# Neighbour features gathered by edge block ahead of the edge loop, scores of two slots in one VectorE instruction

## The chip, the core and the metric

The kernel runs on one core of a Trainium2 chip. The engines are TensorE (PE, with its weight loads PEld), VectorE (DVE), ScalarE (ACT), GpSimd (POOL) and SyncE (SP); SP, ACT and POOL issue DMAs, the indirect ones (gathers by a list of indices) come from POOL. The metric is the device time of one execution in microseconds (us).

## The reference

A graph of 3125 nodes with 16 features each and 100000 edges, sorted by destination. The first layer makes two 16x16 matrices of each edge's 16 attributes, multiplies them with the features of the edge's source node, takes a softmax over the edges of each destination and sums. Two layers of another graph convolution (the sum over neighbours and two small matrices) and a second normalization follow; they are not touched by the change.

```
w_m = (efeat @ W_msg + b_msg).reshape(E, in_f, -1)
w_a = (efeat @ W_attn + b_attn).reshape(E, in_f, -1)
h_src = feat[src][:, :, None]
e1 = w_m * h_src
e2 = w_a * h_src
seg_max = jax.ops.segment_max(e2, dst, num_segments=N)
ex = jnp.exp(e2 - seg_max[dst])
denom = jax.ops.segment_sum(ex, dst, num_segments=N)
attn = ex / denom[dst]
ft = jax.ops.segment_sum(e1 * attn, dst, num_segments=N)
return ft.sum(axis=1)
```

## The kernel before

The edges of a node are cut into groups of up to 8 (`G`), so that a group has 8 slots, of which the last can be empty. 128 groups, one on each partition, make a step. The data here have 111 steps.

**Setup** (0 to 270 us). POOL writes constants. DVE finds where each node's edges start (`less`, `found_i`, L965 to L971), POOL gathers 25 rows of destinations by it (`srow`, L452), DVE works on (L991 to L996), SP sends the start row to DRAM and back onto one partition (`start_row_d`, `r_a`, L312 to L316), DVE does arithmetic on it (L1003 to L1036, `row_ready`), POOL fills tables (L456 to L465, `fill_ready`) and scatters the group table (L470), SP loads it back (`gt`, L328), and DVE scans and turns it into each group's first edge (`est_i`) and the mark of empty slots (`empty`). Beside this ACT and DVE split the edge attributes into bf16 parts (`raise_rows`, `split_rows`) in eight blocks, and ACT writes each into `edge_rows` in DRAM (L781), a row of 102 bf16 values for each edge; the last two hold the index of the edge's source node (L981). SP writes `x_table`: the node features and, behind them, as many rows of ones (L305, L306). `tables_ready` ends the setup.

**Edge loop** (270 to 1868 us). All engines run the same 111 steps, each in its own order, three sets of buffers deep. In a step

- POOL copies the column `t+1` of `est_i` (L481) and fetches by it the 8 edge rows of each group of step t+1 in one indirect DMA (`blk`, L484); for step t it adds `empty` to the source indices in `blk` (`idxi`, L495), so that an empty slot points to a row of ones, and issues one indirect DMA for each of the 8 slots (`hb`, L499), each a gather of 128 rows of 64 bytes;
- PE turns `blk` (L569), multiplies each slot with the weights (L577, 512 columns in one of four PSUM banks) and sums over slots (L585);
- DVE multiplies each slot's product with the gathered features (`score`, L1134, eight instructions of 512 elements), takes the maximum over slots (L1153, L1161, L1167), subtracts it (L1170), and for the step before multiplies messages with the exponentials (`weigh`, L1142);
- ACT copies and exponentiates (L819, L824, L835), SP writes the sums to DRAM (`spill`, L342).

Every instruction of an engine stands in the queue behind the one before it; there is no scheduler, the order is as written. Semaphores count: `h_in` for gathered features, `slot_scored` for scores, `rows_turned`, `sums_kept`, `spill_out`.

**Behind the loop** come two scans (to 2013 us), the joins per node (to about 2300), a division and a normalization, and the two further layers (from 2364).

## Time and profile before

| | us |
|---|---|
| median of 3 runs | 3304.58 (3303.85 to 3307.86) |
| span of the profiled execution | 3304.1 |
| its setup, until POOL's first `estc` | 270.4 |
| its edge loop, from there to DVE's last L1167 | 1581.0 |
| fence load and scans, joins, division | to about 2355 |
| further layers | to 3304.1 |

The profiled execution took 3304.1 us from first to last instruction, 0.5 us under the median of the runs. A profile row gives the line, engine and operation, what is written and read, the shapes and how often, then busy time, mean of one in ns, and the idle time ahead with what ended it ("issue": nothing that the profile shows). A timeline row gives start and duration in us first and, in brackets, the idle time ahead of it.

### The profile page before, as it was taken

The numbers are of one execution on the slowest core, as the hardware profiler recorded it, in microseconds if no ns is written. First come the engines' busy times: TensorE is split into PE (matmuls) and PEld (weight loads), VectorE is DVE, ScalarE is ACT, GpSimd is POOL, SyncE is SP. The second block draws the span as 40 slices with busy tenths as digits, with TensorE's granted clock in tenths as the row PEclk, the third lists the DMA queues.
The fourth block names the chain that finished last, engine by engine and source line by source line (L and its number), as shares of the span: only waits on it lengthen the run. The fifth ranks groups of instructions, "written<-read, shape, count | busy, mean of one in ns | idle before, by whom it ended". The sixth has DMA issues, their size and how long they took to land.

```text
span 3304.1 us, 45362 instructions
## 1 busy us (share of the span) xinstructions
PE 2056.2 (62%) x6488; PEld 812.7 (25%) x6489; DVE 2412.3 (73%) x4260; ACT 1237.7 (37%) x2426; POOL 1238.9 (37%) x1306
## 2 busy tenths in 40 slices
PE   0003777777777777777777403666376666656687
PEld 0001333333333333333333201222022112211233
DVE  3635888888888888888888699898887666656601
ACT  2121322332332323332323102333277777766721
POOL 4035777777777777777777200000000000000000
PEclk9999998999999999999999757999589888988987
DMA  3331111111111111111111203565000000000000
GB/s 128 128 124 43 46 48 44 48 48 48 46 48 46 46 48 48 46 48 47 45 48 48 76 0 110 181 187 172 0 2 1 1 1 1 1 2 1 1 1 3
DMA packets 85993, 166.46 MB, mean 50 GB/s; under 512 B 29032, under 2 KB 45551, under 8 KB 84708
## 3 DMA queue, kind: packets, MB, share of 16 engines
q1 hardware_dynamic: 44066, 103.18, 9.3%
q0 software_dynamic: 37584, 34.07, 5.6%
q10 hardware_dynamic: 4222, 28.14, 2.1%
q14 instruction: 110, 0.90, 0.1%
q8 instruction: 11, 0.18, 0.0%
HBM read 100.19 MB, written 65.60 MB: 50 GB/s over the span
## 4 chain that ended last, share of the span: by engine, by line
POOL 31%; issue 27%; ACT 9%; DVE 9%; PE 9%; DMA 8%; DVEq 3%; ACTq 2%; POOLq 1%; SPq 1%
POOL hb L499 29%; ACT hot_sq L916 5%; DMA md<-group_sums 4%; ACT hot_lo L920 4%; PE bank L724 3%; PE bank L686 2%; DVE mt L1196 2%; PE bank L652 2%; DVEq L288 1%; POOL srow L452 1%; DVE hot_key L1318 1%; ACTq L916 1%; DVE md L1215 1%; POOL idxi L495 1%; DMA edge_rows<-rows 1%
## 5 line engine op out<-in xcount | busy, mean ns | idle before, releaser
L499 POOL DMA_INDIRECT hb<-x_table,idxi x888 | 1005.5, 1132 | 320.1 <-issue 237.5
L585 PE MATMUL bank<-em,identf 128*128 128x512 f32 x1776 | 953.2, 642 | 103.6 <-ACT spb L835 90.3
L1134 DVE TENSOR_TENSOR em<-bank,hb 128x512 f32<-128x512 f32 x888 | 561.4, 685 | 286.2 <-DMA hb<-x_table,idxi 286.2
L686 PE MATMUL bank<-hot_key,hot_lo 128*128 128x500 bf16 x1260 | 443.7, 417 | 218.4 <-ACT hot_lo L920 125.8
L1318 DVE TENSOR_SCALAR hot_key<-iota_key,w,kb 128x500 bf16<-128x500 f16 x1260 | 469.8, 407 | 30.0 <-PE bank L686 15.9
L577 PE MATMUL bank<-wst,eft 100*128 100x512 bf16 x888 | 312.5, 424 | 265.4 <-DVE em L1134 251.0
L585 PEld LDWEIGHTS bank<-em,identf 128*128 128x128 f32 x1776 | 331.7, 203 | 340.2 <-issue 226.6
L916 ACT ACTIVATE hot_sq<-iota_lo,minus_lo 128x128 bf16<-128x128 f16 x840 | 289.5, 392 | 132.1 <-issue 81.7
L824 ACT ACTIVATE em<-em 128x1024 f32<-128x1024 f32 x222 | 234.7, 1057 | 209.2 <-DVE em L1170 148.7
L1142 DVE TENSOR_TENSOR em<-em 128x1024 f32<-128x1024 f32 x222 | 271.5, 1223 | 0.0
L1170 DVE TENSOR_TENSOR em<-em,spb 128x1024 f32<-128x1024 f32 x222 | 262.1, 1222 | 3.8
L1316 DVE TENSOR_SCALAR hot_lo<-iota_lo,minus_lo 128x128 bf16<-128x128 f16 x420 | 106.9, 254 | 212.7 <-issue 153.2
L686 PEld LDWEIGHTS bank<-hot_key,hot_lo 128*128 128x128 bf16 x1260 | 122.9, 98 | 519.9 <-DVE hot_key L1318 489.4
L920 ACT ACTIVATE hot_lo<-hot_sq,one_col 128x256 bf16<-128x256 bf16 x420 | 213.2, 508 | 92.9 <-PE bank L686 50.2
L577 PEld LDWEIGHTS bank<-wst,eft 100*128 100x128 bf16 x888 | 90.8, 102 | 598.8 <-DVE em L1134 444.4
L652 PE MATMUL bank<-md,own_hot 128*128 128x512 f32 x272 | 161.1, 676 | 102.3 <-DVE md L1215 102.1
L814 ACT ACTIVATE blk<-empty 128x8 bf16 (+1 forms) x111 | 26.5, 238 | 497.1 <-DMA blk<-edge_rows,estc 497.1
L819 ACT ACTIVATE eft<-bank 100x1024 bf16<-100x1024 bf16 x111 | 113.6, 1023 | 252.3 <-PE bank L569 159.1
L1161 DVE TENSOR_TENSOR mx<-mx,em 128x512 f32<-128x512 f32 x222 | 153.0, 689 | 0.0
L646 PE MATMUL bank<-identf,mc 128*128 128x128 f32 x272 | 54.3, 283 | 147.6 <-ACT mc L875 147.6
L835 ACT ACTIVATE spb<-bank 128x512 f32<-128x512 f32 x111 | 66.3, 597 | 207.1 <-PE bank L585 148.5
L484 POOL DMA_INDIRECT blk<-edge_rows,estc x112 | 109.3, 976 | 86.1 <-issue 55.3
(250 smaller groups left out, 1871.4 us busy)
## 6 DMA issues: line engine op xcount, KB each, us to landing
md<-group_sums SPq DMA_DIRECT2D x136, 384.0 KB, 3.0
group_sums<-spb SPq DMA_DIRECT2D x111, 384.0 KB
edge_rows<-rows ACTq DMA_DIRECT2D x8, 2490.2 KB
hb<-x_table,idxi POOLq DMA_INDIRECT x888
ef_in<-in_edge_attr ACTq DMA_DIRECT2D x8, 781.2 KB
fence<-fence_d SPq DMA_DIRECT2D x1, 3840.2 KB, 11.5
blk<-edge_rows,estc POOLq DMA_INDIRECT x112
srow<-dst_rows,found_i POOLq DMA_INDIRECT x25
```

The costliest lines, as they stand in the source:

```text
L499: pool.indirect_dma_start(hb[:, b, j, :], None, x_table, bass.IndirectOffsetOnAxis(ap=idxi[:, b, j:j + 1], axis=0)).then_inc(h_in[b], 16)
L577: pe.matmul(bank[j % 4][:, :], eft[:, b, j, :], wst[:, :], start=True, stop=True).then_inc(slot_product, 1)
L585: mm = pe.matmul(bank[5][:, :], identf[:, :], em[:, b, j, :, :].rearrange("p a c -> p (a c)"), start=(j == 0), stop=(j == G - 1))
L652: pe.matmul(bank[4 + b][:, :], own_hot[:, b, :], md[:, b, C:3 * C], start=True, stop=True).then_inc(node_ps, 1)
L686: pe.matmul(bank[b % 4][:, 0:CW], hot_lo[:, q, :], hot_key[:, q, :], start=False, stop=False).then_inc(hot_used, 1)
L824: act.activation(em[:, b, 4 * q:4 * q + 4, 0, :], em[:, b, 4 * q:4 * q + 4, 0, :], ACT.Exp).then_inc(exp_done, 1)
L916: act.activation(hot_sq[:, q - 1, :], iota_lo[:, :], ACT.Square, bias=minus_lo[:, bass.ds(EU * i + q, 1)]).then_inc(sq_done, 1)
L920: act.activation(hot_lo[:, 1:EU, :], hot_sq[:, :, :], ACT.Relu, bias=one_col[:, :], scale=-1.0).then_inc(lo_ready, 1)
L1134: dve.tensor_tensor(em[:, b, j, :, :].rearrange("p a (i o) -> p a i o", i=F), bank[j % 4][:, :].rearrange("p (a i o) -> p a i o", a=2, i=F ...
L1142: dve.tensor_tensor(em[:, b, 4 * q:4 * q + 4, 1, :], em[:, b, 4 * q:4 * q + 4, 1, :], em[:, b, 4 * q:4 * q + 4, 0, :], ALU.mult).then_inc( ...
L1170: dve.tensor_tensor(em[:, b, 4 * q:4 * q + 4, 0, :], em[:, b, 4 * q:4 * q + 4, 0, :], spb[:, b, 0:C].unsqueeze(1).to_broadcast([P, 4, C]), ...
L1318: dve.tensor_scalar(hot_key[:, q, :], iota_key[:, :], w500[:, bass.ds(w, 1)], kb[:, bass.ds(EU * i + q, 1)], ALU.add, ALU.is_equal).then_i ...
```

## The change

The features of the source nodes are no longer gathered slot by slot inside each step.

- The edges are taken in 98 blocks (`NBLK`) of 1024 in their own order. `collect(n)` gathers the features of one block with eight indirect DMAs from `x` into one of three stages (`h_stage`); the indices come straight from `src` (`load_src`, `src_ring`). SP writes the stage to `h_rows` in DRAM (`keep_h`). 19 blocks (`HPRE`) are collected in the setup, three before the `srow` gathers, eight before `row_ready`, one before the scatter and seven behind it; the other 79 in steps 0 to 95, one in five of each six steps (`blocks_by`).
- Since the edges of a group follow each other, one indirect DMA then fetches the features of all 8 slots of a step (`hb`, in `fetch`), with the same index as `blk`. The first 96 steps are written out on POOL and SP, in the others the old copy of the index stays (`fetch_late`).
- Empty slots: POOL multiplies `hb` with `real` and adds `empty` (`raise_empty`, two instructions of 128x128), and DVE waits for `h_ready`. Row 99 of the weights holds -BIG for them.
- SP's write-backs stand in its queue among the DMAs of the setup, and in the loop ahead of the spill of three steps before.
- Scores and messages lie as (i, a, o) instead of (a, i, o), so that one DVE instruction of 1024 elements scores two slots from two neighbouring PSUM banks (`quad`), and PE signals every second product. ACT, the joins and the division read the new order.
- `edge_rows` has 100 values a row instead of 102, `x_table`, its ones and the copy of the indices (L981) go, and two iotas move behind `x1_ready`.

```diff
+PAIRS = G // 2
...
-ROW = 102
+ROW = 100
...
-FLAG = N
+HBLK = G * P
+NBLK = -(-E // HBLK)
+HST = 3
+HCH = 7
+HPRE = 19
+HSTEPS = 96
...
-        x_table = dram("x_table", (FLAG + N, F), F32)
+        h_rows = dram("h_rows", (NBLK * HBLK, F), F32)
...
+        quad = ctx.enter_context(nc.psum_tensor("quad", [P, 4, 512], F32))
...
-        iota_key = sb("iota_key", [P, CW], FP16)
-        iota_lo = sb("iota_lo", [P, P], FP16)
...
+        src_ring = sb("src_ring", [P, 2, HCH, G], I32)
+        h_stage = sb("h_stage", [P, HST, G, F], F32)
...
-        em = sb("em", [P, 3, G, 2, C], F32, level1)
-        mx = sb("mx", [P, 2, C], F32, level1)
+        em = sb("em", [P, 3, G, F, 2, F], F32, level1)
+        mx = sb("mx", [P, 2, F, F], F32, level1)
...
-        empty = sb("empty", [P, T * G], I32, level1)
+        real = sb("real", [P, T * G], BF16, level1)
+        empty = sb("empty", [P, T * G], BF16, level1)
...
+        src_ld = [sem(f"src_ld{i}") for i in range(2)]
+        h_got = [sem(f"h_got{i}") for i in range(HST)]
+        h_out = [sem(f"h_out{i}") for i in range(HST)]
+
+        def blocks_by(t):
+
+            return min(NBLK, HPRE + 5 * t // 6)
+
+        def load_src(eng, c):
+
+            n = min(HCH, E // HBLK - c * HCH)
+            part = src[c * HCH * HBLK:(c * HCH + n) * HBLK].rearrange("(c p j) -> p c j", p=P, j=G)
+            eng.dma_start(src_ring[:, c % 2, 0:n, :], part).then_inc(src_ld[c % 2], 16)
+            if n < HCH:
+                rest = E - (c * HCH + n) * HBLK
+                eng.dma_start(src_ring[0:rest // G, c % 2, n, :], src[E - rest:E].rearrange("(p j) -> p j", j=G)).then_inc(src_ld[c % 2], 16)
...
+        def scores(b, j, n):
+
+            return em[:, b, j:j + n, :, 0, :].rearrange("p j i o -> p (j i) o")
+
+        def messages(b, j, n):
+
+            return em[:, b, j:j + n, :, 1, :].rearrange("p j i o -> p (j i) o")
...
+            def keep_h(n):
+
+                sp.wait_ge(h_got[n % HST], 16 * G * (n // HST + 1))
+                sp.dma_start(h_rows[n * HBLK:(n + 1) * HBLK, :].rearrange("(p j) f -> p (j f)", p=P),
+                             h_stage[:, n % HST, :, :].rearrange("p j f -> p (j f)")).then_inc(h_out[n % HST], 16)
+                if n % HCH == HCH - 1 and n // HCH + 2 < NBLK // HCH:
+                    load_src(sp, n // HCH + 2)
+
+            for n in range(5):
+                keep_h(n)
...
+            keep_h(5)
...
+            for n in range(6, 10):
+                keep_h(n)
...
+            for n in range(10, 12):
+                keep_h(n)
...
+            for n in range(12, 14):
+                keep_h(n)
...
+            keep_h(14)
...
-            for t in range(3):
-                spill(t, t)
+            for n in range(15, HPRE):
+                keep_h(n)
+            for t in range(HSTEPS):
+                for n in range(blocks_by(t), blocks_by(t + 1)):
+                    keep_h(n)
+                if t >= 3:
+                    spill(t - 3, t % 3)
             n3 = loops(sp)
...
+            sp.wait_ge(fetched, 1)
...
+            def collect(n):
+
+                k, c = n % HST, n // HCH
+                if n % HCH == 0:
+                    pool.wait_ge(src_ld[c % 2], 16 * (c // 2 + 1) if (c + 1) * HCH * HBLK <= E else 16 * (c // 2 + 2))
+                ge(pool, h_out[k], 16 * (n // HST))
+                for j in range(G):
+                    pool.indirect_dma_start(h_stage[:, k, j, :], None, x,
+                                            bass.IndirectOffsetOnAxis(ap=src_ring[:, c % 2, n % HCH, j:j + 1], axis=0)).then_inc(h_got[k], 16)
+
+            for n in range(3):
+                collect(n)
...
+            for n in range(3, 11):
+                collect(n)
...
+            collect(11)
...
+            for n in range(12, HPRE):
+                collect(n)
...
+            def fetch(t, b, index, rows):
 
                 ge(pool, rows_turned, t - 2)
                 pool.nop(nofuse=True)
+                pool.indirect_dma_start(blk[:, b, :, :].rearrange("p g r -> p (g r)"), None, edge_rows,
+                                        bass.IndirectOffsetOnAxis(ap=index, axis=0)).then_inc(blk_in[b], 16)
+                ge(pool, slot_scored, PAIRS * (t - 2))
+                pool.nop(nofuse=True)
+                pool.indirect_dma_start(hb[:, b, :, :].rearrange("p g f -> p (g f)"), None, h_rows[0:rows, :],
+                                        bass.IndirectOffsetOnAxis(ap=index, axis=0)).then_inc(h_in[b], 16)
+
+            def fetch_early(t):
+
+                if t < NBLK:
+                    pool.wait_ge(h_out[t % HST], 16 * (t // HST + 1))
+                fetch(t, t % 3, est_i[:, t:t + 1], HBLK * (t + 1 if t < NBLK - 2 else NBLK))
+
+            def fetch_late(t, b):
+
                 pool.tensor_copy(estc[:, b:b + 1], est_i[:, bass.ds(t, 1)]).then_inc(pool_step, 1)
-                pool.wait_ge(pool_step, base + 1 if isinstance(t, int) and t == 0 else base + 2 * t)
+                pool.wait_ge(pool_step, base + t - HSTEPS)
                 pool.nop(nofuse=True)
-                pool.indirect_dma_start(blk[:, b, :, :].rearrange("p g r -> p (g r)"), None, edge_rows,
-                                        bass.IndirectOffsetOnAxis(ap=estc[:, b:b + 1], axis=0)).then_inc(blk_in[b], 16)
-
-            def gather(t, b, i):
-
-                pool.wait_ge(blk_in[b], 16 * (i + 1))
-                ge(pool, h_in[b], 16 * G * i)
-                ge(pool, slot_scored, G * (t - 2))
+                fetch(t, b, estc[:, b:b + 1], HBLK * NBLK)
+
+            def raise_empty(t, b, i):
+
+                pool.wait_ge(h_in[b], 16 * (i + 1))
                 pool.nop(nofuse=True)
-                srcs = blk[:, b, :, :].rearrange("p g r -> p (g r)").bitcast(I32)\
-                    .rearrange("p (g r) -> p g r", g=G)[:, :, KROWS // 2]
-                pool.tensor_tensor(idxi[:, b, :], srcs, empty[:, bass.ds(t * G, G)], ALU.add).then_inc(pool_step, 1)
-                pool.wait_ge(pool_step, base + 2 * t + 3)
+                pool.tensor_tensor(hb[:, b, :, :], hb[:, b, :, :],
+                                   real[:, bass.ds(t * G, G)].unsqueeze(2).to_broadcast([P, G, F]), ALU.mult).then_inc(h_masked, 1)
+                pool.wait_ge(h_masked, t + 1)
                 pool.nop(nofuse=True)
-                for j in range(G):
-                    pool.indirect_dma_start(hb[:, b, j, :], None, x_table,
-                                            bass.IndirectOffsetOnAxis(ap=idxi[:, b, j:j + 1], axis=0)).then_inc(h_in[b], 16)
-
+                pool.tensor_tensor(hb[:, b, :, :], hb[:, b, :, :],
+                                   empty[:, bass.ds(t * G, G)].unsqueeze(2).to_broadcast([P, G, F]), ALU.add).then_inc(h_ready, 1)
+
+            fetch_early(0)
+            for t in range(HSTEPS):
+                fetch_early(t + 1)
+                raise_empty(t, t % 3, t // 3)
+                for n in range(blocks_by(t), blocks_by(t + 1)):
+                    collect(n)
             n3 = loops(pool)
             n4 = joins(pool)
-            fetch(0, 0)
-            for t in range(3):
-                fetch(t + 1, (t + 1) % 3)
-                gather(t, t, 0)
-            with pool.Fori(1, n3) as i:
+            pool.wait_ge(h_out[(NBLK - 1) % HST], 16 * ((NBLK - 1) // HST + 1))
+            with pool.Fori(HSTEPS // 3, n3) as i:
                 for b in range(3):
-                    fetch(3 * i + b + 1, (b + 1) % 3)
-                    gather(3 * i + b, b, i)
+                    fetch_late(3 * i + b + 1, (b + 1) % 3)
+                    raise_empty(3 * i + b, b, i)
             pool.wait_ge(blk_in[0], 16 * n3 + 16)
...
+            pool.wait_ge(x1_ready, 1)
+            pool.iota(iota_key[:, :], [[1, CW]], base=0, channel_multiplier=0, allow_small_or_imprecise_dtypes=True).then_inc(iotas_ready, 1)
...
-                ge(pe, slot_scored, G * t + j - 3)
-                pe.matmul(bank[j % 4][:, :], eft[:, b, j, :], wst[:, :], start=True, stop=True).then_inc(slot_product, 1)
+                if j % 2 == 0:
+                    ge(pe, slot_scored, PAIRS * t + j // 2 - 1)
+                mm = pe.matmul(bank[j % 4][:, :], eft[:, b, j, :], wst[:, :], start=True, stop=True)
+                if j % 2 == 1:
+                    mm.then_inc(slot_product, 1)
...
-                dve.tensor_copy(rows[:, b, :, :].rearrange("p e r -> p (e r)").bitcast(I32)
-                                .rearrange("p (e r) -> p e r", e=PC)[:, :, KROWS // 2], src_i[:, c, :]).then_inc(rows_done, 1)
...
-            link(dve.tensor_scalar(empty[:, :], eslot[:, :, :].rearrange("p t g -> p (t g)"), float(FLAG), None, ALU.mult))
+            link(dve.tensor_tensor(eslot[:, :, :], eslot[:, :, :], gm[:, 2, :].unsqueeze(2).to_broadcast([P, T, G]), ALU.is_lt))
+            link(dve.tensor_copy(real[:, :], eslot[:, :, :].rearrange("p t g -> p (t g)")))
+            link(dve.tensor_scalar(empty[:, :], real[:, :], -1.0, 1.0, ALU.mult, ALU.add))
...
-            def score(t, b, j):
-
-                dve.wait_ge(slot_product, G * t + j + 1)
-                dve.tensor_tensor(em[:, b, j, :, :].rearrange("p a (i o) -> p a i o", i=F),
-                                  bank[j % 4][:, :].rearrange("p (a i o) -> p a i o", a=2, i=F),
-                                  hb[:, b, j, :].unsqueeze(1).unsqueeze(3).to_broadcast([P, 2, F, F]),
+            def score(t, b, q):
+
+                dve.wait_ge(slot_product, PAIRS * t + q + 1)
+                dve.tensor_tensor(em[:, b, 2 * q:2 * q + 2, :, :, :].rearrange("p j i a o -> p (j i) (a o)"),
+                                  quad[:, 2 * q % 4:2 * q % 4 + 2, :].rearrange("p j (i c) -> p (j i) c", i=F),
+                                  hb[:, b, 2 * q:2 * q + 2, :].rearrange("p j i -> p (j i)").unsqueeze(2).to_broadcast([P, 2 * F, 2 * F]),
                                   ALU.mult).then_inc(slot_scored, 1)
...
-                dve.tensor_tensor(em[:, b, 4 * q:4 * q + 4, 1, :], em[:, b, 4 * q:4 * q + 4, 1, :],
-                                  em[:, b, 4 * q:4 * q + 4, 0, :], ALU.mult).then_inc(weighed, 1)
+                dve.tensor_tensor(messages(b, 4 * q, 4), messages(b, 4 * q, 4), scores(b, 4 * q, 4), ALU.mult).then_inc(weighed, 1)
...
-                dve.wait_ge(h_in[b], 16 * G * (i + 1))
+                dve.wait_ge(h_ready, t + 1)
...
-                for j in range(5):
-                    score(t, b, j)
-                dve.wait_ge(slot_scored, G * t + 4)
-                dve.tensor_tensor(mx[:, :, :], em[:, b, 0:2, 0, :], em[:, b, 2:4, 0, :], ALU.max).then_inc(max_taken, 1)
+                for q in range(3):
+                    score(t, b, q)
+                halves = mx[:, :, :, :].rearrange("p j i o -> p (j i) o")
+                dve.wait_ge(slot_scored, PAIRS * t + 2)
+                dve.tensor_tensor(halves, scores(b, 0, 2), scores(b, 2, 2), ALU.max).then_inc(max_taken, 1)
+                score(t, b, 3)
                 for q in range(2):
-                    for j in ((5, 6), (7,))[q]:
-                        score(t, b, j)
```

On POOL, one step of the loop before (`estc`, `idxi` are indices, `blk` the edge rows, `hb` the features):

```order
L481 COPY estc<-est_i 128x1
L484 DMA blk<-edge_rows,estc 128x816
L495 TENSOR_TENSOR idxi<-blk,empty 128x8
L499 DMA hb<-x_table,idxi 128x16 x8
L481 COPY estc<-est_i 128x1
```

and after, a step with a block and the start of the next:

```order
L548 DMA blk<-edge_rows,est_i 128x800
L552 DMA hb<-h_rows,est_i 128x128
L572 TENSOR_TENSOR hb<-hb,real 128x128
L576 TENSOR_TENSOR hb<-hb,empty 128x128
L506 DMA h_stage<-in_x,src_ring 128x16 x8
L548 DMA blk<-edge_rows,est_i 128x800
L552 DMA hb<-h_rows,est_i 128x128
```

Eight gathers stay in a step that has a block; a fetch and a tensor_tensor came in, the copy and the small tensor_tensor went.

On POOL in the setup, before (`srow` rows of destinations, `gid` to `er` the fills):

```order
L447 MEMSET rows 125x200
L452 DMA srow<-dst_rows,found_i 128x256 x25
L428 IOTA gid 128x120
L428 IOTA eslot 128x960
L428 IOTA kst 1x148
L459 MEMSET wflag 1x256
L460 MEMSET wflag 1x256
L461 MEMSET fence_end 1x2
L462 MEMSET minus 1x2
L463 MEMSET er 128x896
L464 MEMSET er 128x896
L470 DMA group_table<-pay,slot_i 15360x4 x25
```

and after, first up to the fills:

```order
L497 MEMSET rows 125x200
L506 DMA h_stage<-in_x,src_ring 128x16 x24
L514 DMA srow<-dst_rows,found_i 128x256 x25
L506 DMA h_stage<-in_x,src_ring 128x16 x64
L481 IOTA gid 128x120
```

then, on the same engine, from the last fill to the first fetch of the loop:

```order
L528 MEMSET er 128x896
L506 DMA h_stage<-in_x,src_ring 128x16 x8
L535 DMA group_table<-pay,slot_i 15360x4 x25
L506 DMA h_stage<-in_x,src_ring 128x16 x56
L548 DMA blk<-edge_rows,est_i 128x800
```

The gathers stand between the steps of the setup's own work, all in one queue.

## Rows read from the trace of the kernel before

**Rows 1.** The page: busy times, slices of POOL and DVE, the chain
```profile
PE 2056.2 (62%) x6488; PEld 812.7 (25%) x6489; DVE 2412.3 (73%) x4260; ACT 1237.7 (37%) x2426; POOL 1238.9 (37%) x1306
...
DVE  3635888888888888888888699898887666656601
...
POOL 4035777777777777777777200000000000000000
...
POOL hb L499 29%; ACT hot_sq L916 5%; DMA md<-group_sums 4%; ACT hot_lo L920 4%; PE bank L724 3%; PE bank L686 2%; DVE mt L1196 2%; PE bank L652 2%; DVEq L288 1%; POOL srow L452 1%; DVE hot_key L1318 1%; ACTq L916 1%; DVE md L1215 1%; POOL idxi L495 1%; DMA edge_rows<-rows 1%
```

**Rows 2.** The page's costliest group: count, busy us, mean ns, idle before
```profile
L499 POOL DMA_INDIRECT hb<-x_table,idxi x888 | 1005.5, 1132 | 320.1 <-issue 237.5
```

**Rows 3.** Timeline of POOL in one step of the loop, and its last step
```profile
1005.93 0.20 POOL L481 COPY estc<-est_i 128x1 int32 x1
1006.90 0.98 POOL L484 DMA_INDIRECT blk<-edge_rows,estc  x1 [0.77 <-POOL estc L481]
...
1008.85 0.96 POOL L499 DMA_INDIRECT hb<-x_table,idxi  x1 [0.75 <-POOL idxi L495]
1010.12 0.95 POOL L499 DMA_INDIRECT hb<-x_table,idxi  x1 [0.30 <-issue]
...
1014.11 1.43 POOL L499 DMA_INDIRECT hb<-x_table,idxi  x1 [0.30 <-issue]
...
1020.12 0.20 POOL L481 COPY estc<-est_i 128x1 int32 x1
...
1825.60 0.35 POOL L481 COPY estc<-est_i 128x1 int32 x1
```

**Rows 4.** Timeline of DVE: scores, shift and last maximum of the last two steps
```profile
1828.60 3.08 DVE L1134 TENSOR_TENSOR em<-bank,hb 128x512 f32<-128x512 f32 x5 [2.69 <-DMA hb<-x_table,idxi]
...
1837.92 2.36 DVE L1170 TENSOR_TENSOR em<-em,spb 128x1024 f32<-128x1024 f32 x2
1842.55 3.08 DVE L1134 TENSOR_TENSOR em<-bank,hb 128x512 f32<-128x512 f32 x5 [2.26 <-DMA hb<-x_table,idxi]
...
1851.41 0.43 DVE L1167 TENSOR_TENSOR spb<-mx 128x256 f32<-128x256 f32 x1
```

**Rows 5.** Busy times in the loop, with granted clock of PE, DMA share, GB/s
```profile
284.00:1854.00 1570.00, 1202.85 (x3727) 503.52 (x3728) 1290.55 (x1774) 466.27 (x658) 1150.97 (x1212) 0.93 0.18 47
```

**Rows 6.** Timeline of POOL in the setup
```profile
38.41 2.41 POOL L452 DMA_INDIRECT srow<-dst_rows,found_i  x1 [30.07 <-DVE found_i L971]
...
47.00 0.95 POOL L452 DMA_INDIRECT srow<-dst_rows,found_i  x1 [0.30 <-issue]
...
73.18 0.95 POOL L452 DMA_INDIRECT srow<-dst_rows,found_i  x1 [0.30 <-issue]
153.27 0.23 POOL L428 IOTA gid<- 128x120 f32 x1 [79.15 <-DVE r_c L1036]
...
171.90 1.02 POOL L470 DMA_INDIRECT group_table<-pay,slot_i  x1 [13.36 <-issue]
...
270.40 0.18 POOL L481 COPY estc<-est_i 128x1 int32<-128x1 int32 x1 [62.98 <-issue]
```

**Rows 7.** Timeline of DVE in the setup, and one row of ACT
```profile
20.55 10.34 DVE L965 TENSOR_TENSOR less<-rl_b,node_id 128x9775 bf16<-128x9775 f32 x1
...
38.03 1.82 DVE L980 TENSOR_TENSOR resid<-ef_in,rows 125x1600 f32<-125x1600 f32 x1
...
91.74 6.83 DVE L991 TENSOR_TENSOR less<-srow,node_id 128x6400 bf16<-128x6400 int32 x1 [8.20 <-DMA srow<-dst_rows,found_i]
...
102.09 4.21 ACT L772 ACTIVATE rows<-ef_in 125x4800 bf16<-125x4800 f32 x1 [20.40 <-DMA edge_rows<-rows]
```

**Rows 8.** Groups of POOL: its other instructions, mean ns of one
```profile
L495 POOL TENSOR_TENSOR idxi<-blk,empty 128x8 int32<-128x8 int32 x111 | 23.1, 208 | 2.8 <-DMA blk<-edge_rows,estc 0.4
...
L428 POOL IOTA eslot<- 128x960 f32 x1 | 1.8, 1823 | 0.1
...
L428 POOL IOTA iota_key<- 128x500 f16 x1 | 0.5, 547 | 0.1
...
L443 POOL TENSOR_SCALAR_AFFINE_SELECT identf<-identf 128x128 f32<-128x128 f32 x1 | 0.3, 292 | 0.2 <-POOL identf L442 0.2
...
L428 POOL IOTA iota_lo<- 128x128 f16 x1 | 0.2, 238 | 0.1
```

**Rows 9.** Timeline of DVE before the further layers
```profile
2364.56 0.26 DVE L1316 TENSOR_SCALAR hot_lo<-iota_lo,minus_lo 128x128 bf16<-128x128 f16 x1 [7.05 <-issue]
```

103 lines of the change are left out of this document (52 added, 51 removed).

## The prediction

> **What bounds the kernel now.** I read the page first: the busy times, the 40 slices and the chain [rows 1]. No engine is over 73% of the span, but in slices 3 to 23, the edge loop, POOL shows 7 in every slice and DVE 8, and the chain puts its largest share, 29%, on one POOL line, L499. Then the costliest groups [rows 2]: L499 is 888 indirect DMAs of 1.132 us each, with 0.36 us before each that is nearly all "issue". That is 8 gathers for each of 111 steps. So I looked at POOL's timeline over one step [rows 3]: L481 starts at 1005.93 and again at 1020.12, and between them POOL has no idle time that another engine ends. The first L481 of the run is at 270.40 [rows 6] and the last, the 112th, at 1825.60 [rows 3]; the first two are 2.0 us apart, so 110 pitches take 1553.2 us, **14.12 us for one step**. DVE in the same place [rows 4]: the step from 1828.60 ends at 1840.28, 11.7 us of work back to back, then it idles 2.3 us for the DMA of `hb`. PE is busy 1202.85 us in 1570 us, 10.8 us a step at a mean granted clock of 0.93 [rows 5]. POOL's own instruction stream binds the loop, DVE is 2.4 us a step behind it, PE about 3.
>
> The setup (0 to 270 us) is another matter: POOL stands idle there 30.07 + 79.15 + 13.36 + 62.98 = 185.6 us [rows 6].
>
> **What the change does to POOL.** Before, POOL issues 25 + 25 indirect DMAs in the setup, then 112 of L484 and 888 of L499: 1050. After: the same 50, 98 blocks x 8 = 784 gathers, and two fetches (`blk`, `hb`) for each of 112 steps, 224: 1058. The number does not fall; what changes is when they are issued. 19 blocks (152 gathers) go ahead of the loop, 79 blocks (632) into its first 96 steps, none into the last 15. In exchange every step gets two POOL tensor_tensor instructions of 128x128, chained by `h_masked`, for a copy and a tensor_tensor of 128x8.
>
> **Price of a gather.** 0.95 us and 0.30 us of issue, 1.25 us, when nothing disturbs it [rows 3, 6]. Beside the `em` and `mx` instructions of DVE it takes 1.43 us instead. The mean of 1.132 against 0.945 is 0.187 x 8 = 1.5 us a step of disturbance. In the setup the pattern is plain: DVE's L980 runs from 38.03 to 39.85, and POOL's gather that starts at 38.41 takes 2.41 us, so it ends 0.97 us after it [rows 6, 7]. A gather that starts while DVE runs an instruction with two SBUF inputs does its 0.95 us after that one's end. The Trainium skill (SBUF — State Buffer, Who interferes with whom) says that such an instruction contends with a GpSimd instruction that reads SBUF and the later one fully blocks, which the two rows bear out; it infers that the writing of a DMA's descriptors is left alone by tensor_tensor, and by that the setup would come out some 40 us shorter than I take below. The rows speak against that part.
>
> **The first 96 steps, per step.** Gathers: 632/96 = 6.58 x 1.25 = 8.23. The two fetches: 0.98 + 0.30 each [rows 3], 2.56. Disturbance by DVE, whose work in SBUF is the same as before: 1.5. The two tensor_tensors of 128 elements: no such row exists. POOL's 128x8 one takes 0.208, an affine_select of 128x128 0.292, an iota of 960 elements 1.823, 1.9 ns an element [rows 8]. Lower end 0.29; by the iota's slope 0.21 + 120 x 0.0019 = 0.44; with that slope for each of two inputs 0.67. I take 0.50, somewhat above the middle one since each reads a second operand: 1.0 for both. The Trainium skill (GPSIMD Engine Reference, 3.1 Elementwise — side-by-side cycle accounting) gives 2.6 cycles an element for this instruction; an estimate from it is 0.28 us for the 128 elements, and no run here shows it yet. Between the two stands a semaphore: L481 to L484 and L495 to L499 show 0.77 and 0.75 where an undisturbed issue shows 0.30 [rows 3], so 0.45. Both read SBUF and write into `hb`, so each can meet a running DVE instruction: DVE spends 7.3 of 14 us on such ones, a wait of up to 1.2, on average 0.2 each: 0.4. Waits that find their semaphore set: 0.1. Sum 8.23 + 2.56 + 1.5 + 1.0 + 0.45 + 0.4 + 0.1 = **14.2 us**, against 14.12: the gathers that leave the step are paid back by the second fetch and the two tensor_tensors. With the low ends (0.29, a gap of 0.1, no blocking) 13.3; with the high ends (0.67, blocking 0.8) 15.0.
>
> The new waits do not add. SP must write a block back (`keep_h`) ahead of a spill, and DVE's L1167 must have the spill of three steps before; that puts DVE some 5 to 8 us behind POOL's last gather of a step, but POOL's own waits look back a whole step further (`slot_scored` of two steps before), so it does not stall, also after the one step in six with no gathers.
>
> **The last 15 steps.** POOL needs about 5 us, so DVE or PE binds. DVE: 11.7 us now. Scores of two slots in one instruction: five of 512 take 3.08, so 0.60 each; one of 1024 from SBUF takes 1.18 to 1.22 (two of L1170 in 2.36) [rows 4], so a pair costs 1.13 to 1.22 where two cost 1.20: -0.3 to +0.1 us a step. PE at 10.8 us with its order of waits is close. I take **12.0**, range 11.5 to 13: 15 x (14.12 - 12.0) = 32 us gained. In the first 96 steps the paired scores gain nothing, since DVE waits there anyhow.
>
> **The setup.** POOL's work ahead of the first fetch: 7 us of constants (8.3 less three instructions removed) [rows 6, 8], 202 indirect DMAs x 1.25 = 252.5, the fills 5.3 (153.27 to 158.54): 265 us. On top the DVE instructions in whose shadow a gather now stands: L965 alone runs 10.34 us [rows 7] from 20.55, when block 1 is being gathered, L991 6.83 us, the single-partition arithmetic ahead of row 153.27 has some 17 us of two-input work, and each L980 and L984 costs about 1 us: 40 together. Then POOL stands still at times. The transfers themselves go slowly while the `edge_rows` blocks are written: the last `srow` gather is issued at 73.18, ends at 74.1, and its data is there at 91.74 [rows 6, 7]; ACT waits 20.40 us for such a write [rows 7]. Blocks 3 to 5 queue behind `srow`, only three stages exist, and SP puts five write-backs ahead of `start_row_d` and four ahead of `g0_row_d`, so the chain of the group table slips too: first by about 15 us (block 1 and 2 delay `srow` from 38.4 to 53), then more. I allow 25 us. First fetch at 265 + 40 + 25 = **330 us** against 270.4. Lower end 305 (POOL never waits), upper end 345.
>
> **Sum.** POOL ends the gathers of step 95 at 330 + 96 x 14.2 = 1693. DVE's L1167 of that step follows about 7 us later, 1700, and fifteen steps of 12.0 end at 1880, against 1851.41 for the last L1167 now [rows 4]: +29 us. Behind the loop nothing changes in size: the joins and the division work on as many elements in another order. The two iotas moved behind `x1_ready` take 0.55 + 0.24 us [rows 8] and lie under a DVE gap of 7.05 us [rows 9]: 0. If that gap were not there they would cost 0.8. The profiled execution has a span of 3304.1 us, 0.5 under the median of 3304.58. So 3304.6 + 29 = **3333 us**.
>
> **Rivals.**
> A. Cheap POOL instructions: step 13.4 instead of 14.2, from a tensor_tensor of 0.35 or less and little blocking: 96 x 0.8 = 77 less, 3256 us. For it: DVE has idle time where they can fall. It decides below 13.9 us a step: then the change is faster.
> B. The setup hides the early gathers, as the 185.6 us of idle against 152 x 1.25 = 190 suggest. First fetch at 300, step 14.1: 3294 us. It needs that long DVE instructions do not hold a gather up; [rows 6, 7] show that they do. The Trainium skill's inference on tensor_tensor, above, is this case.
> C. POOL and DVE hold each other up by the tensor_tensors: 15.0 a step: 96 x 0.8 = 77 more, 3410 us.
> D. The scores in pairs as such: if POOL were no bound, they would bring at most 0.3 x 111 = 33 us. POOL binds in 96 steps, so 5 us at best; no case of its own, it is in the 12.0.
>
> **Chances.** Forecast (3311 to 3365) 0.42, C and its neighbourhood 0.20, A 0.20, B 0.10, and 0.08 for a near cancelling of terms. About 0.2% (6.6 us) is what a measurement of this kernel tells from no change. Slower by more: 0.60; within: 0.10; faster by more: 0.30. The range runs from A to just short of C: 3250 to 3395.
>
> **What would show it.** In the trace after: the first `blk` fetch near 330 us; a pitch of `blk` fetches that alternates between about 16 us (five steps) and 5 (one), mean 14.2, up to step 95, then 12; POOL without idle ended by another engine there; POOL's 128x128 tensor_tensor at 0.5; DVE's pair at 1.2; the gather near 20.6 us lasting until L965's successor ends. A first fetch before 305, a tensor_tensor under 0.35 or a mean pitch under 13.9 would turn the sign; a mean pitch over 15 means case C.

## The result and the profile after

The changed kernel takes **3277.88 us** (median of 4 runs, 3275.5 to 3286.85) against 3304.22 us for the kernel before, timed beside it on the same chip. The ratio is 0.9924, interval 0.991 to 0.9938: faster by 0.8%, where the prediction had 3333 us and 0.60 for slower. The time lies in the prediction's range (3250 to 3395), the sign is wrong. The profiled execution has a span of 3276.4 us, so its sums can be held against those of [rows 1 to 9].

The page of the changed kernel, its busy times, the slices of POOL and the chain (beside [rows 1]):

```profile
PE 2002.4 (61%) x6488; PEld 811.5 (25%) x6489; DVE 2407.7 (73%) x3809; ACT 1223.8 (37%) x2426; POOL 1396.3 (43%) x1327
...
POOL 8877777888778778888754000000000000000000
...
POOL h_stage L506 22%; ACT hot_sq L1006 4%; ACT hot_lo L1010 4%; DMA md<-group_sums 3%; POOL hb L552 3%; POOL blk L548 3%; PE quad L812 3%; PE quad L774 2%; DVE mt L1286 2%; PE bank L740 2%; POOL hb L576 2%; POOL hb L572 1%; DVE em L1223 1%; PE bank L673 1%; DVEq L319 1%
```

POOL is busy from the first slice on; GpSimd's lines, the gathers L506 above all, are still the largest part of the chain. Now the groups of POOL in the first 96 steps (325.6 to 1622 us): count, busy us, mean ns of one, idle before and what ended it.

```profile
L506 POOL DMA_INDIRECT h_stage<-in_x,src_ring x632 | 689.6, 1091 | 184.8 <-issue 180.0 <-DVE em L1223 3.4
L552 POOL DMA_INDIRECT hb<-h_rows,est_i x96 | 119.5, 1245 | 30.7 <-issue 30.7
L548 POOL DMA_INDIRECT blk<-edge_rows,est_i x96 | 113.9, 1186 | 28.5 <-issue 28.4
L576 POOL TENSOR_TENSOR hb<-hb,empty 128x128 f32<-128x128 f32 x95 | 60.2, 634 | 13.9 <-POOL hb L572 0.4
L572 POOL TENSOR_TENSOR hb<-hb,real 128x128 f32<-128x128 f32 x95 | 53.7, 565 | 1.6
```

Busy and idle together are the whole stretch, and only 4 us of the idle time is ended by another engine: POOL's stream binds these steps, as forecast. Four rows of its timeline set the ends: the first fetch, that of step 96, the one behind it, and the last fetch of all.

```profile
325.61 0.94 POOL L548 DMA_INDIRECT blk<-edge_rows,est_i  x1 [0.30 <-issue]
...
1622.05 0.95 POOL L548 DMA_INDIRECT blk<-edge_rows,est_i  x1 [0.30 <-issue]
...
1628.30 1.10 POOL L548 DMA_INDIRECT blk<-edge_rows,estc  x1 [0.88 <-POOL estc L563]
...
1786.55 1.16 POOL L548 DMA_INDIRECT blk<-edge_rows,estc  x1 [0.82 <-POOL estc L563]
```

(1622.05 - 325.61) / 96 = **13.50 us a step**, where 14.2 was forecast; the kernel before has 14.12 over its whole loop and 14.00 counted in this way. VectorE's timeline, its maxima of step 95 and of the last step (beside [rows 4]):

```profile
1640.73 0.62 DVE L1255 TENSOR_TENSOR spb<-mx 128x256 f32<-128x256 f32 x1
...
1818.64 0.41 DVE L1255 TENSOR_TENSOR spb<-mx 128x256 f32<-128x256 f32 x1
```

The loop's last maximum stands at 1818.6 instead of 1851.4, 33 us earlier; what comes behind it takes 1457 us instead of 1452.

POOL's gathers in the setup (0 to 325.6 us):

```profile
L506 POOL DMA_INDIRECT h_stage<-in_x,src_ring x152 | 194.5, 1279 | 48.1 <-issue 47.5 <-DMA h_rows<-h_stage 0.6
```

Only 0.6 us of the idle time ahead of them is a wait for a write-back: POOL's own stream binds the setup as well.

### The profile page after: what moved, and what is told of

Same layout as the page of the kernel before. It is cut to its first block, busy times and chain, and to the rows that moved or that the text cites. A ratio compares the mean times of both kernels' runs of the same rounds, so it can differ in the third digit from the quotient of the medians.

```text
span 3276.4 us, 43067 instructions
## 1 busy us (share of the span) xinstructions
PE 2002.4 (61%) x6488; PEld 811.5 (25%) x6489; DVE 2407.7 (73%) x3809; ACT 1223.8 (37%) x2426; POOL 1396.3 (43%) x1327
## 4 chain that ended last, share of the span: by engine, by line
POOL 33%; issue 25%; DVE 11%; PE 10%; ACT 9%; DMA 5%; DVEq 3%; ACTq 2%; SPq 1%; POOLq 0%
POOL h_stage L506 22%; ACT hot_sq L1006 4%; ACT hot_lo L1010 4%; DMA md<-group_sums 3%; POOL hb L552 3%; POOL blk L548 3%; PE quad L812 3%; PE quad L774 2%; DVE mt L1286 2%; PE bank L740 2%; POOL hb L576 2%; POOL hb L572 1%; DVE em L1223 1%; PE bank L673 1%; DVEq L319 1%
## 5 line engine op out<-in xcount | busy, mean ns | idle before, releaser
L673 PE MATMUL bank<-em,identf 128*128 128x512 f32 x1776 | 932.2, 629 | 89.0 <-ACT spb L924 89.0
L506 POOL DMA_INDIRECT h_stage<-in_x,src_ring x784 | 884.0, 1128 | 232.9 <-issue 227.4
L1223 DVE TENSOR_TENSOR em<-quad,hb 128x1024 f32<-128x1024 f32 x444 | 526.1, 1215 | 201.7 <-PE quad L663 143.0
L774 PE MATMUL quad<-hot_key,hot_lo 128*128 128x500 bf16 x1260 | 434.5, 407 | 229.3 <-ACT hot_lo L1010 135.7
L663 PE MATMUL quad<-wst,eft 100*128 100x512 bf16 x888 | 276.7, 417 | 47.8 <-DVE em L1223 47.6
L1231 DVE TENSOR_TENSOR em<-em 128x1024 f32<-128x1024 f32 x222 | 280.5, 1264 | 0.0
L1260 DVE TENSOR_TENSOR em<-em,spb 128x1024 f32<-128x1024 f32 x222 | 267.8, 1247 | 3.8
L774 PEld LDWEIGHTS quad<-hot_key,hot_lo 128*128 128x128 bf16 x1260 | 122.4, 97 | 522.5 <-DVE hot_key L1410 493.9
L654 PE MATMUL bank<-identb,blk 128*100 128x128 bf16 x888 | 85.3, 251 | 237.3 <-ACT blk L903 237.3
L908 ACT ACTIVATE eft<-bank 100x1024 bf16<-100x1024 bf16 x111 | 113.7, 1024 | 232.6 <-PE bank L654 211.0
L663 PEld LDWEIGHTS quad<-wst,eft 100*128 100x128 bf16 x888 | 89.2, 106 | 310.7 <-issue 163.4
L1249 DVE TENSOR_TENSOR mx<-mx,em 128x512 f32<-128x512 f32 x222 | 157.8, 711 | 0.1
L654 PEld LDWEIGHTS bank<-identb,blk 128*100 128x100 bf16 x888 | 72.8, 148 | 313.5 <-ACT blk L903 175.1
```

Source lines behind the costliest of these rows:

```text
L506: pool.indirect_dma_start(h_stage[:, k, j, :], None, x, bass.IndirectOffsetOnAxis(ap=src_ring[:, c % 2, n % HCH, j:j + 1], axis=0)).then_i ...
L663: mm = pe.matmul(bank[j % 4][:, :], eft[:, b, j, :], wst[:, :], start=True, stop=True)
L673: mm = pe.matmul(bank[5][:, :], identf[:, :], em[:, b, j, :, :, :].rearrange("p i a o -> p (i a o)"), start=(j == 0), stop=(j == G - 1))
L774: pe.matmul(bank[b % 4][:, 0:CW], hot_lo[:, q, :], hot_key[:, q, :], start=False, stop=False).then_inc(hot_used, 1)
L1223: dve.tensor_tensor(em[:, b, 2 * q:2 * q + 2, :, :, :].rearrange("p j i a o -> p (j i) (a o)"), quad[:, 2 * q % 4:2 * q % 4 + 2, :].rearra ...
L1231: dve.tensor_tensor(messages(b, 4 * q, 4), messages(b, 4 * q, 4), scores(b, 4 * q, 4), ALU.mult).then_inc(weighed, 1)
```

## Experiments

"Last maximum" below is the end of the last `spb` instruction of VectorE in the profile, "behind" what follows it up to the end. Ratios are to the kernel before, timed beside it on the same chip (3298.9 to 3300.2 us for the runs named by a label).

| kernel | time us | ratio (95%) | first fetch | pitch, 96 steps | mean gather there | last maximum | behind |
|---|---|---|---|---|---|---|---|
| before | 3304.2 | 1 | 271.4 | 14.00 | 1.133 | 1851.8 | 1452 |
| changed | 3277.9 | 0.9924 (0.991-0.9938) | 325.6 | 13.50 | 1.091 | 1819.1 | 1457 |
| `again` | 3273.4 | 0.9917 (0.9901-0.9934) | 326.5 | 13.42 | 1.090 | 1812.3 | 1462 |
| `pairs_only` | 3281.2 | 0.9946 (0.9927-0.9966) | 273.1 | 13.74 | 1.099 | 1822.8 | 1458 |
| `no_pairs` | 3301.6 | 1.0008 (0.9993-1.0023) | 325.6 | 13.53 | 1.095 | 1826.7 | 1472 |
| `shift` | 3281.9 | 0.9936 (0.9914-0.9959) | 325.5 | 13.49 | 1.089 | 1823.8 | 1457 |
| `three_tt` | 3308.9 | 1.0033 (1.002-1.0045) | 324.4 | 13.86 | 1.049 | 1853.1 | 1454 |
| `one_add` | 3169.6 | 0.961 (0.9594-0.9626) | 326.9 | 12.43 | 1.071 | 1717.5 | 1450 |
| `dve_add` | 3164.5 | 0.9598 (0.9582-0.9614) | 325.7 | 12.36 | 1.129 | 1709.7 | 1450 |
| `psum_less` | 3263.8 | 0.9896 (0.9879-0.9914) | 315.6 | 13.47 | 1.095 | 1807.3 | 1453 |
| `reduce_max` | 3275.6 | 0.9923 (0.9903-0.9944) | 326.3 | 13.25 | 1.109 | 1818.8 | 1457 |
| `best` | 3289.2 | 0.9964 (0.9951-0.9977) | 317.2 | 13.35 | 1.143 | 1833.7 | 1453 |
| `dve_psum` | 3157.9 | 0.9576 (0.9557-0.9595) | 315.4 | 12.35 | 1.123 | 1699.2 | 1457 |

(The pitch of the kernel before is here that of its first 96 steps from fetch to fetch; the mean gather is busy time over count in that stretch, in us. The edits below are shortened to what they change.)

**Is it GpSimd's stream that counts?** `three_tt` issues the multiplication twice:

```diff
+ pool.tensor_tensor(hb, hb, real, ALU.mult).then_inc(h_masked, 1)
+ pool.wait_ge(h_masked, 2 * t + 1)
  pool.tensor_tensor(hb, hb, real, ALU.mult).then_inc(h_masked, 1)
```

> The changed kernel with GpSimd's multiplication by `real` done twice in each step (L572, the value is the same). Theory P (GpSimd's own stream sets the pitch of the first 96 steps, every instruction of it counts 96 times): one more tensor_tensor of 0.565 us and a semaphore gap of 0.14 us (the mean of L572 and the mean idle time ahead of L576 in the trace of the changed kernel) make 0.70 x 96 = +68 us, 3345 us (3325 to 3365), and nothing in the last 15 steps, where VectorE is the full engine. Rival D (VectorE and TensorE, or the spills, set the pitch and GpSimd is only carried along): 3278 to 3285 us.

`one_add` issues one instruction in place of two:

```diff
- tensor_tensor(hb, hb, real, ALU.mult); wait; tensor_tensor(hb, hb, empty, ALU.add)
+ tensor_tensor(hb, hb, floor, ALU.add)      # floor = 16 * empty
```

> The changed kernel with one tensor_tensor in place of the two: 16 x `empty` is added to the features and nothing is multiplied, so an empty slot's factor is 16 plus a feature instead of 1, positive all the same while the features are below 16 in size, and its score is still of the size of -BIG. Theory P: one tensor_tensor and its semaphore gap less in each of 96 steps, 0.70 x 96 = -68 us, 3210 us (3195 to 3230). Rival D: within 10 us of the changed kernel's 3278.

`dve_add` moves that one addition to the head of VectorE's step; the late fetches then wait for `h_ready` of three steps before:

```diff
- pool: raise_empty(t, b, i)
+ dve: dve.tensor_tensor(hb, hb, floor, ALU.add).then_inc(h_ready, 1)
+ pool: pool.wait_ge(h_ready, t - 2)          # ahead of the copy into estc
```

> The same single addition, issued by VectorE at the head of its step instead of by GpSimd; GpSimd then has only its 8 gathers and two fetches. Theory P: GpSimd's step falls by 1.34 us (1.20 of the two tensor_tensors and 0.14 of the gap) from 13.50 to 12.16 us; VectorE's busy time per step rises from 11.35 (1090.07 / 96) by 0.2 to 0.4. GpSimd and VectorE then lie close together and wait for each other at times: a pitch of 12.2 to 12.6, so 3278 - 96 x (0.9 to 1.3) = 3153 to 3192 us, plus 15 late steps x 0.3 = 5 us; I take 3175. If the mutual disturbance (gathers of 1.09 instead of 0.95 us) gets worse since VectorE is busier, the upper end. Rival D: VectorE's step is what counts and grows by 0.2 to 0.4 us: 3300 to 3315 us.

Against the 3274 to 3278 us of the changed kernel the three measured +31 to +35, -104 to -108 and -109 to -113 us. The direction is theory P's each time, and rival D of these three texts (GpSimd only carried along) is out. The sizes are not 68 us a piece: 3308.9 and 3169.6 us lie outside both ranges that were given for them (3325 to 3365, 3195 to 3230), 3164.5 lies inside its own. POOL's groups over its 96 steps in `one_add`, then in `three_tt`:

```profile
L506 POOL DMA_INDIRECT h_stage<-in_x,src_ring x632 | 676.6, 1070 | 180.8 <-issue 166.3 <-DVE em L1219 7.9 <-DMA hb<-h_rows,est_i 2.4
L552 POOL DMA_INDIRECT hb<-h_rows,est_i x96 | 112.9, 1176 | 34.6 <-issue 27.7 <-DMA hb<-h_rows,est_i 6.3 <-DVE em L1219 0.6
L548 POOL DMA_INDIRECT blk<-edge_rows,est_i x96 | 100.2, 1044 | 26.9 <-issue 26.7
L572 POOL TENSOR_TENSOR hb<-hb,floor 128x128 f32<-128x128 f32 x95 | 59.8, 630 | 1.6
```

```profile
L506 POOL DMA_INDIRECT h_stage<-in_x,src_ring x632 | 662.7, 1049 | 188.2 <-issue 183.0 <-DVE em L1227 3.7
L552 POOL DMA_INDIRECT hb<-h_rows,est_i x96 | 112.7, 1174 | 30.1 <-issue 29.8 <-DMA hb<-h_rows,est_i 0.3
```

In `one_add` the instruction and its gap give 0.70 x 96 = 68 us, and the indirect DMAs are shorter as well: 13.0 + 6.6 + 13.7 = 33 us; 101 in all, and the last maximum is 101.6 us earlier. In `three_tt` the third instruction adds some 67 us and the gathers give 27 back (1.091 to 1.049). In these kernels the stream's sum is the pitch; what I had taken as constant, the 1.5 us a step of disturbance, is not. That shows in `dve_add` too. It differs from `one_add` in that the last tensor_tensor, 59.8 us of POOL's stream, went over to VectorE; yet the last maximum comes only 8 us earlier (1709.7 against 1717.5), since its gathers are 37 us longer in sum (713.8 against 676.6) and the idle time ahead of them 12 us:

```profile
L506 POOL DMA_INDIRECT h_stage<-in_x,src_ring x632 | 713.8, 1129 | 192.6 <-issue 190.7 <-DVE em L1213 1.2 <-PE bank L644 0.3
```

Nearly all of the gain over the changed kernel is thus that of leaving out the multiplication.

**What does each half of the change bring?** `pairs_only` is the kernel before with the new order of `em`, `mx` and the weights and with the paired scores, the gathers left as they were:

```diff
- for j in range(G): score(t, b, j)           # em[:, b, j] <- bank[j % 4] * hb[:, b, j]
+ for q in range(PAIRS): score(t, b, q)       # em[:, b, 2q:2q+2] <- quad[:, 2q%4:2q%4+2] * hb[:, b, 2q:2q+2]
```

> The kernel before with one part of the change alone: the order of em, mx and the weights by (input feature, kind, output feature) and two slots scored by one instruction of VectorE; the gathers stay where they were, after their step's index addition. Theory P (GpSimd binds the loop of the kernel before too, at its 14 us and more a step): the pairs give nothing, 3304 us (3298 to 3310). Rival D: the pairs are where the change's gain comes from: 3278 us or less. In between would mean that VectorE's lighter step disturbs the gathers less.

It took 18 us off, two thirds of the whole gain, between theory P (3298 to 3310) and rival D (3278 or less). Its gathers and scores over the run:

```profile
L509 POOL DMA_INDIRECT hb<-x_table,idxi x888 | 972.7, 1095 | 320.1 <-issue 236.4 <-POOL idxi L505 83.3 <-PE bank L579 0.3
...
L1148 DVE TENSOR_TENSOR em<-quad,hb 128x1024 f32<-128x1024 f32 x444 | 523.7, 1218 | 279.9 <-DMA hb<-x_table,idxi 264.1 <-PE quad L588 15.4
```

Beside [rows 2] the idle time ahead of the gathers is the same, 320.1, and their busy time is 1005.5 - 972.7 = 32.8 us less; the last maximum comes 29 us earlier. VectorE waits for the gathers as before. So the paired scores work through the length of the gathers. Which ones were shortened can be counted (400 to 1600 us): in the kernel before 170 of 680 gathers start beside the weighing and take 1.43 us on average, here 27 of 692. (Behind the loop `pairs_only` takes 6 us more than the kernel before. The boundaries told of below cost it 8 us more in sum, for the same instructions, which hides that much of its gain.) `no_pairs` is the reverse, the changed kernel with single scores:

```diff
- PE: wait for and count two slots at a time; DVE: 4 scores of 128x1024
+ PE: wait for and count one slot at a time;  DVE: 8 scores of 128x512
```

> The changed kernel with one slot scored per instruction of VectorE again (888 of 0.6 us pitch instead of 444 of 1.2), all else as changed. The runs so far have split the theory. Theory G (GpSimd's stream sets the pitch, and its gathers are lengthened by VectorE's instructions with both inputs in SBUF, while beside a score, which reads PSUM, they take 0.95 us): the pairs act on the time through the gathers alone; in the kernel before they brought the mean gather from 1.132 to 1.098 us, so here the gathers go from 1.09 to 1.12 to 1.14: +0.03 to +0.05 x 8.6 indirect DMAs x 96 = +25 to +40 us over the changed kernel (ratio to before 1.000 to 1.005). Theory N (the prediction's: the pairs are worth at most 5 us in steps that GpSimd binds): 0 to +5 us (ratio 0.992 to 0.994).

3301.6 us, inside theory G's range, and by luck: the trace shows the same gathers as with pairs (1.095 against 1.091 us), the same pitch (13.53 against 13.50), the last maximum 7.6 us later, and 15 us more *behind* the loop, where both kernels execute the same instructions. VectorE's timeline at a boundary between two groups of windows, in `no_pairs` and in the changed kernel:

```profile
2596.76 0.25 DVE L1406 TENSOR_SCALAR hot_lo<-iota_lo,minus_lo 128x128 bf16<-128x128 f16 x1 [15.46 <-issue]
```

```profile
2592.83 0.25 DVE L1408 TENSOR_SCALAR hot_lo<-iota_lo,minus_lo 128x128 bf16<-128x128 f16 x1 [13.23 <-issue]
```

There are eight such boundaries, and 8 x 2.2 = 18 us, enough for the 15. `again` and `shift` settle what they are:

> The changed kernel itself once more, beside the kernel before on the same chip, to see how far the profiles of one program agree. If the part behind the edge loop is the program's own, it repeats: last maximum at 1819, 1457 us behind it, 14.5 us over each of the eight boundaries between groups of windows (start of one hot_lo to the next), ratio 0.992. If the difference between 1452 and 1472 us behind the loop is chance from execution to execution, these numbers move by 5 us or more here.

```diff
+ for k in range(16): dve.nop(nofuse=True)    # VectorE, ahead of the first group of windows
```

> The kernel with gathers ahead and single scores (ratio 1.0008), plus 16 empty instructions on VectorE right ahead of the counting windows, so that the windows' code lies elsewhere in VectorE's instructions; nothing else. There VectorE took 16.6 to 17.1 us over each of eight boundaries between groups of windows, against 14.5 in the changed kernel and 14.2 in the kernel before. Theory J (what the boundary costs depends on where the loop's code lies): it becomes another number, 14 to 15.5 us, and the time falls by 10 to 22 us to 3280 to 3292, with the edge loop's end where it was (last maximum at 1827). Rival (the scores' form or chance makes the part behind the loop longer): 16.8 us again, and 3298 to 3304 us.

`again` repeats the boundaries (14.4 to 14.8 us from one `hot_lo` to the next); its parts otherwise differ from the first profile's by up to 7 us, which is how closely two profiles of one program agree. `shift`, with sixteen instructions *more* than `no_pairs`, is 20 us faster:

```profile
2597.87 0.25 DVE L1406 TENSOR_SCALAR hot_lo<-iota_lo,minus_lo 128x128 bf16<-128x128 f16 x1 [12.67 <-issue]
```

Theory J holds so far as this one displacement shows it: what lies behind the loop takes 1457 us instead of 1472 with the same work in it. How the place acts was not looked into. `shift` is the fair kernel with single scores: 0.9936, its last maximum at 1823.8. Gathering ahead without pairs brings 21 us; pairs on top of it bring 4 to 8 us by the times, 5 to 11 by the last maximum, of which the late steps explain 3.4 (12.09 against 11.86 us each). The intervals of the ratios overlap (0.9914 to 0.9959, 0.991 to 0.9938), so that the times alone do not tell this from nothing. Each half alone brings 18 to 21 us, both together 25 to 27.

**What lengthens a gather?**

```diff
- less[...] <- rl_b (SBUF)             is_lt node_id (SBUF)
+ less[...] <- bank[0] (PSUM, as TensorE left it) is_lt node_id (SBUF)
```

> The changed kernel with one operand of the comparison in the setup (L1055, 10.34 us) read from PSUM, where TensorE left it, instead of from its copy in SBUF; the same values. Theory G: the gather that runs in the comparison's shadow (11.0 us from its start to the next one's) takes 1.25 us as the others do, GpSimd reaches its first fetch of the loop at 316 instead of 325.6 us, and the time falls by up to 9.7 us: -10 to -5. Rival (any instruction of VectorE holds a gather, or the comparison does so through its length alone): the gather stays at 11 us and the time within 2 us of the changed kernel's. Third case: the gather is freed, but the chain of tables that VectorE works on was as late as GpSimd: the first fetch stays at 320 or later.

The timelines of POOL and VectorE in the setup of the changed kernel, then of `psum_less`:

```profile
20.58 10.65 POOL L506 DMA_INDIRECT h_stage<-in_x,src_ring  x1 [0.30 <-issue]
...
20.07 10.34 DVE L1055 TENSOR_TENSOR less<-rl_b,node_id 128x9775 bf16<-128x9775 f32 x1
```

```profile
20.60 0.94 POOL L506 DMA_INDIRECT h_stage<-in_x,src_ring  x1 [0.30 <-issue]
21.84 0.94 POOL L506 DMA_INDIRECT h_stage<-in_x,src_ring  x1 [0.30 <-issue]
...
31.82 2.71 POOL L506 DMA_INDIRECT h_stage<-in_x,src_ring  x1 [0.31 <-issue]
...
20.64 10.34 DVE L1055 TENSOR_TENSOR less<-quad,node_id 128x9775 bf16<-128x9775 f32 x1
31.02 2.70 DVE L1058 TENSOR_TENSOR less<-less 128x4850 bf16<-128x4850 bf16 x1
```

The comparison takes 10.34 us in both. Reading two inputs from SBUF it holds one gather for its whole length; with one input in PSUM eight gathers run beside it at 0.94 us each, and the next instruction with both inputs in SBUF holds one again. A held gather ends 0.82 us after the comparison (31.23 against 30.41) and 0.81 us after the fold (34.53 against 33.72). Since the length of the comparison is the same in both kernels, its length alone is not the cause. The first fetch comes at 315.6 instead of 325.6, the ratio is 0.9896 against 0.9917 and 0.9924: some 7 to 9 us, as expected.

For the loop I sorted the gathers (L506, 400 to 1600 us) by the instruction of VectorE that runs at their start. Changed kernel: beside a score, which has one input in PSUM, 212 gathers, all of 0.94 to 0.99 us; beside nothing 119, the same; beside a maximum 70 (L1249) of 1.33 on average, 30 (L1242) of 1.24 and 29 (L1255) of 1.16; beside the weighing (L1231) 43 of 1.64; beside the subtraction (L1260) 82 of 1.10. Where in the instruction a gather starts decides its length: the 43 all end 0.81 to 0.86 us after the weighing that they meet, and of the 82 the 48 that start in the last 0.14 us of a subtraction take 0.94 to 0.96 us, as if alone. `reduce_max` takes one of these kinds away:

```diff
- three maxima of 128x512 into mx, one of 128x256 into spb
+ dve.tensor_reduce(spb, em[:, b, :, :, 0, :] as (i, o, slot), AX.X, ALU.max)
```

> The changed kernel with the four maxima of a step (tensor_tensor with both inputs in SBUF, 3 x 0.68 and 0.41 us) replaced by one tensor_reduce over the eight slots, which has one input; the same values. From the setup's reductions (3.47 us for 3200 elements, 0.57 for 400) it takes 2.3 us, as long as the four together. Theory G: the 101 of 585 gathers that begin beside a maximum and take 1.23 to 1.33 us instead of 0.95 are freed, 0.06 x 6.6 per step and a little for the two fetches: 0.4 to 0.6 us a step, -38 to -58 us (ratio to before 0.975 to 0.981). If the same gathers then fall beside the weighing (both inputs in SBUF, 1.2 us) instead, half of it. Rival (what lengthens a gather is VectorE's busy time as such, or its start and end, not where it reads): within 10 us of the changed kernel.

```profile
L1246 DVE TENSOR_REDUCE spb<-em 128x256 f32<-128x2048 f32 x94 | 342.9, 3648 | 16.4 <-DMA group_sums<-spb 16.3
...
L506 POOL DMA_INDIRECT h_stage<-in_x,src_ring x633 | 701.6, 1108 | 188.9 <-issue 184.7 <-DVE em L1223 4.0
```

It was no faster (0.9923), where theory G had 0.975 to 0.981; the rival's number came true. The part of the theory on where VectorE reads held: 187 gathers start beside the reduction, which has one input, and all of them take 0.94 to 0.99 us. But the reduction takes 3.65 us and not 2.3, and the weighing and the subtraction now stand in rows of two, so the gathers that start beside them, 146, take 1.60 and 1.63 on average, and the mean gather is 1.109 instead of 1.091 us. With a longer step of VectorE the late steps cost more, too: 13.2 us each instead of 11.86.

> Three edits together: the addition of 16 x `empty` on VectorE in place of the two instructions of GpSimd, the reduction for the maximum, and the comparison that reads PSUM. Theory G: against the kernel with the addition on VectorE alone (ratio 0.960) GpSimd's step, 12.36 us there with gathers of 1.129, falls by 0.5 us and the setup by 7 us: -55 us, ratio 0.943. But VectorE (11.6 us a step of work) and TensorE then lie within 0.3 us of GpSimd, and waits come up on both sides: I take -30 us, ratio 0.951. Rival: 0.960, no gain over that kernel.

`best` missed by most: 0.9964, slower than every case given for it (0.943 to 0.960). VectorE's step, 13.1 us of work with the reduction and the addition, became the bound; POOL now waits for it ahead of the fetches of its first 96 steps, and the late steps take 13.65 us:

```profile
L552 POOL DMA_INDIRECT hb<-h_rows,est_i x96 | 97.5, 1015 | 114.1 <-DVE em L1213 87.5 <-issue 26.6
```

Without the reduction:

> The addition of 16 x `empty` on VectorE and the comparison that reads PSUM, without the reduction that took 3.65 us instead of 2.3. The two act in different stretches, so they add: 3164.5 - 9 = 3155 us (3148 to 3162), ratio 0.957; the first fetch at 316 and a pitch of 12.35 us. If VectorE and not GpSimd's stream now sets the loop, the setup's 9 us would still be kept, since the whole loop starts earlier; only if the tables were the later ones is the gain under 3 us.

`dve_psum` is the fastest kernel here, 3157.9 us, ratio 0.9576, and its parts add up as expected (first fetch 315.4, pitch 12.35).

## Why the prediction was wrong

**The bound** was right: in the first 96 steps POOL's stream, in the last 15 VectorE (idle 0.03 us a step there), and the pitch alternates as told.

**First fetch**: 330 forecast, 325.6 measured, but two of its terms were wrong and cancelled, which is luck. The 40 us for gathers in VectorE's shadow were 59 (the 202 indirect DMAs over 0.945 us each), and the 25 us in which POOL would stand still were about 2: the longest idle time ahead of a gather is 2.06 us, and the write-backs cost 0.6. Rival B (300) fell; of its 26 us `psum_less` gives back 10 by freeing the gathers beside one comparison.

**The step of the first 96**, 14.2 forecast against 13.50, is where the prediction failed: 0.70 x 96 = 67 us, more than twice the +29 us of the forecast. By its own terms, per step:

| term | forecast | measured |
|---|---|---|
| gathers, undisturbed | 8.23 | 8.15 |
| two fetches, undisturbed | 2.56 | 2.51 |
| disturbance | 1.5 | 0.96 (gathers) + 0.54 (fetches) |
| two tensor_tensors, with blocking | 1.4 | 1.19 |
| gap for the semaphore | 0.45 | 0.14 |
| waits | 0.1 | 0.02 |

The term that was most wrong is the gap for the semaphore: 0.45 us forecast, 0.14 measured, 30 us over 96 steps; the two tensor_tensors follow with 1.4 against 1.19, 20 us. With both as measured the sum would have forecast a faster kernel. I had read 0.75 us ahead of a DMA that uses an index just written [rows 3] as the price of a semaphore between any two of POOL's instructions. The kernel before had a row of the pair that was to be priced, one compute instruction of POOL behind another that it depends on, with 0.17 us between them:

```profile
5.22 0.29 POOL L443 TENSOR_SCALAR_AFFINE_SELECT identf<-identf 128x128 f32<-128x128 f32 x1 [0.17 <-POOL identf L442]
```

In the changed kernel's timeline the second tensor_tensor follows 0.14 us after the first, and the gather after it has 0.15 us of issue, not 0.30:

```profile
1032.03 0.95 POOL L548 DMA_INDIRECT blk<-edge_rows,est_i  x1 [0.30 <-issue]
1033.28 0.94 POOL L552 DMA_INDIRECT hb<-h_rows,est_i  x1 [0.30 <-issue]
1034.24 0.41 POOL L572 TENSOR_TENSOR hb<-hb,real 128x128 f32<-128x128 f32 x1
1034.79 0.67 POOL L576 TENSOR_TENSOR hb<-hb,empty 128x128 f32<-128x128 f32 x1
1035.62 1.79 POOL L506 DMA_INDIRECT h_stage<-in_x,src_ring  x1 [0.15 <-issue]
```

Undisturbed the tensor_tensor takes 0.41 (0.50 taken); with blocking 0.565 and 0.634 on average, so that the blocking of both together, 0.38, is the 0.4 that was taken. `one_add` bears the sizes out: the instruction and the gap that it leaves out were worth 0.70 us a step, where the prediction's terms would make them 1.15.

The disturbance agrees in sum only: 1.5 us was that of eight gathers a step, and there are 6.58 here with 0.96 us; the two fetches, for which nothing was set down, add 0.54. The low end of the step is also wrong as a sum: its terms make 13.1, not 13.3. Rival A's pitch (13.4) and sign are what came, but not its reason: it wanted a tensor_tensor of 0.35 us or less and little blocking, and it kept the gap that failed.

**VectorE's lag** was the second miss: step 95's maximum stands 18.7 us behind the fetch of step 96 (1640.7 - 1622.05), not 7. Of that, 6.3 us are a slip in the count: 96 pitches from the first fetch end at the fetch of step 96, and POOL's step 95 comes behind it (to 1628.30). The lag proper is 12.4 us. **The last steps** came as forecast, 11.86 against 12.0. The sum by the measured terms: 1880 - 4 (first fetch) - 67 (pitch) + 12 (lag) - 2 (late steps) = 1819, where the last maximum is. **Behind the loop**: 0 forecast, +5 us measured in the first profile; of the same size as the difference between two profiles of this program (1457 and 1462). The eight boundaries of the windows have 3 us of it (105 us in sum against 102); the rest is not explained.

**The pairs** (the prediction's rival D, at most 5 us where POOL binds): 4 to 8 us by the times beside `shift`, about what was said for this kernel. As a general statement it was wrong: in the old order of gathers the same pairs brought 18 us although VectorE had time to spare, since they changed which gathers fall beside instructions with two inputs in SBUF. Why they do so there and hardly here isn't settled beyond the counts (beside the weighing 170 gathers became 27 there; here it is 75 in `shift` and 43 with pairs, while more fall beside maxima): no run controls the places of the gathers singly.

## What to carry to other kernels

Where GpSimd's stream of indirect DMAs binds, count its instructions and look at what VectorE does beside each: here instructions with both inputs in SBUF lengthened gathers and those with one input in PSUM did not, so an edit of an engine that is not the bound moved the time. Take the price of a semaphore from the same kind of pair (compute to compute, or index write to DMA): the trace before may have one, as here. And before two programs are compared by their times, compare stretches in which they do the same: here sixteen empty instructions ahead of a loop were worth 15 us behind the edge loop, over half of what the change itself brought.

## What the runs showed of the hardware that was not expected

- A gather beside VectorE: 0.94 to 0.99 us for all 212 that start beside a score with one input in PSUM and all 187 beside a reduction with one input, up to 2.0 us beside a tensor_tensor of the edge loop with both inputs in SBUF (`shift`), 10.65 us beside one of 10.34.
- A held gather ends 0.81 to 0.86 us after the VectorE instruction that it met (all 43 beside the weighing in the changed kernel).
- The effect is mutual: of the 75 weighings of VectorE (L1231) that overlap a tensor_tensor of GpSimd between 325 and 1640 us, 42 take 1.41 to 1.45 us, and none of the 115 others takes over 1.22.
- A maximum over eight slots as tensor_reduce, 2048 elements with 2 KB from one to the next, takes 3.65 us; 3200 elements in a row took 3.47 in the setup, by which it would have been 2.3.
- From one pass to the next of an outer loop VectorE stood idle for 15.5 or 12.7 us ("issue") with the same instructions, changed by 16 empty ones ahead of the loop; in the other kernels it was 12.6 to 14.0.
- One tensor_tensor more or less on GpSimd was worth +31 to +35 and -104 to -108 us, not the same amount: the indirect DMAs around it became shorter in both.
